# Rebuilt prologue of a two-layer Flamingo kernel: norm statistics on TensorE and ScalarE, another load order, products moved behind the routers, 16-bit tables

## What is computed

```
x = x + tanh(g_xattn[0]) * (_layernorm(x) * rs)     # rs: scan, r = 0.9 r + ctx*ctx along each sequence
x = x + tanh(g_ffn[0])   * _L0_ffn_ref(_layernorm(x), Wg, W_in, W_out)
x = x + tanh(g_xattn[1]) * _L1_xattn_ref(_layernorm(x), ctx, ctx, Wq, bq, Wk, bk, Wv, bv, mask, 1)
x = x + tanh(g_ffn[1])   * _L1_ffn_ref(_layernorm(x), gate_w, w1, w2)

# _L0_ffn_ref: S = 2048 tokens, E = 8 experts, K = 2, capacity C = 640
logits = xf @ Wg;  probs = softmax(logits);  top_vals, top_idx = top_k(probs, K)
loc = place of the token in its expert's list (cumsum of one-hots);  keep = loc < C
buf[e, loc] = token row;  hid = buf @ W_in;  hid = gelu(a) * g;  out_e = hid @ W_out
y = sum over K of out_e[e, loc] * gates
```

## Time and profile before

| | us |
|---|---|
| three runs | 569.64, 570.64, 571.45 |
| median | 570.64 |
| span of the profiled execution | 573.6 |
| TensorE busy in that span | 532.9 (93%) |
| first expert product starts | 76.33 |

### The profile page before, as it was taken

One profiled execution on the slowest core, in us unless ns is written; L12 is line 12 of the kernel. 1 busy time (PEld: TensorE's weight loads), 2 busy tenths in 40 slices (PEclk: granted clock), 3 DMA queues, 4 the chain that ended last, 5 costly groups with the idle time before them and its releaser, 6 DMA issues.

```text
span 573.6 us, 12551 instructions
## 1 busy us (share of the span) xinstructions
PE 532.9 (93%) x4079; PEld 508.9 (89%) x4080; DVE 335.6 (59%) x796; ACT 321.8 (56%) x670; POOL 251.9 (44%) x284
## 2 busy tenths in 40 slices
PE   2899889999999999998996989999999999999993
PEld 1789789999999999986785879999999999999993
DVE  2888845765655675475677865464626463543631
ACT  3573345665656675435577646565646574654742
POOL 2400366664455542314000354556565546654654
PEclk9997699999999999979999899999999999999998
DMA  8944253445245443362033343644454545362333
GB/s 251 382 172 149 74 160 105 152 153 169 91 152 172 119 160 110 119 221 75 0 110 129 77 157 69 191 118 113 113 122 96 143 110 119 48 193 45 42 51 44
DMA packets 52454, 72.76 MB, mean 127 GB/s; under 512 B 7200, under 2 KB 43936, under 8 KB 52416
## 3 DMA queue, kind: packets, MB, share of 16 engines
q1 hardware_dynamic: 40752, 50.34, 26.7%
q0 software_dynamic: 11664, 21.94, 17.2%
HBM read 51.54 MB, written 20.73 MB: 126 GB/s over the span
## 4 chain that ended last, share of the span: by engine, by line
PE 80%; DVE 9%; DMA 4%; ACT 3%; issue 2%; POOL 1%; DVEq 0%; SPq 0%; POOLq 0%; ACTq 0%
PE PA L1684 27%; PE PD L1684 18%; PE PC L1684 17%; PE PB L1515 3%; PE PC L1515 2%; PE PD L1515 2%; PE PB L1696 2%; DMA xg<-xn_rows,row_x 2%; PE PB L1873 2%; DVE stats L990 1%; DMA cx<-ctx 1%; PE PA L1515 1%; PE PA L1549 1%; PE PB L1509 1%; DVE xs L1043 1%
## 5 line engine op out<-in xcount | busy, mean ns | idle before, releaser
L1684 PE MATMUL PA<-xhi,whi 128*128 128x256 f32 (+1 forms) x440 | 128.6, 292 | 4.2 <-issue 2.1
L1684 PE MATMUL PA<-xhi,wlo 128*128 128x256 f32 (+1 forms) x440 | 125.8, 286 | 0.0
L1684 PE MATMUL PA<-xlo,whi 128*128 128x256 f32 (+1 forms) x440 | 125.7, 286 | 0.0
L1250 DVE TENSOR_TENSOR hlo<-cT_all,hhi 128x512 fp32r<-128x512 f32 x78 | 54.2, 694 | 111.8 <-ACT hhi L937 111.7
L935 ACT ACTIVATE cT_all<-PA 128x512 f32<-128x512 f32 x78 | 46.6, 597 | 93.2 <-PE PA L1684 93.1
L609 POOL DMA_INDIRECT out<-ys,row_o x38 | 63.5, 1670 | 75.6 <-DVE ys L1456 41.5
L1684 PEld LDWEIGHTS PA<-xhi,whi 128*128 128x128 f32 x440 | 84.2, 191 | 5.6 <-issue 4.5
L1684 PEld LDWEIGHTS PA<-xlo,whi 128*128 128x128 f32 x440 | 84.2, 191 | 0.0
L1684 PEld LDWEIGHTS PA<-xhi,wlo 128*128 128x128 f32 x440 | 84.1, 191 | 0.0
L1684 PE MATMUL PD<-whi,hhi 128*128 128x256 f32 x284 | 81.1, 285 | 0.4 <-DVE wlo L1202 0.4
L1684 PE MATMUL PD<-whi,hlo 128*128 128x256 f32 x284 | 80.4, 283 | 0.0
(11 more groups left out here) (269 smaller groups left out, 1205.6 us busy)
## 6 DMA issues: line engine op xcount, KB each, us to landing
raw<-w SPq DMA_DIRECT2D x16, 1024.0 KB, 5.7
raw<-L_ffn_W_in SPq DMA_DIRECT2D x8, 1024.0 KB, 5.2
raw<-L_ffn_W_out SPq DMA_DIRECT2D x8, 512.0 KB
y_rows<-ys SPq DMA_DIRECT2D x8, 512.0 KB, 8.0
xn_rows<-xn SPq DMA_DIRECT2D x8, 512.0 KB, 3.5
xs<-x SPq DMA_DIRECT2D x4, 512.0 KB, 6.5
cx<-ctx SPq DMA_DIRECT2D x4, 512.0 KB, 7.0
ys<-y_rows SPq DMA_DIRECT2D x4, 512.0 KB, 4.6
```

The lines of the kernel that those rows point to most:

```text
L1250: return dve.tensor_tensor(dst, src, hi.bitcast(F32), ALU.subtract)
L1684: mm = pe.matmul(dst, a[k], b[k], start=(first and k == 0 and a is lhs_hi and b is rhs_hi), stop=(last and k == n - 1 and a is lhs_lo))
```

## The change

- **Norm statistics of layer 0's second norm.** The router's weights get a ninth column of -1/256, so `rows_router` also gives minus the mean. ACT squares the rows with that mean as bias and sums them (`squares1`), then takes the root (`root1`). `norm_stats(1, q)` on DVE goes.
- **Normalising.** POOL makes the coefficients and normalises quads 0 and 1, DVE quads 2 and 3 (`normalised1`, the first behind `one_hots(0)`, the second behind `pick`); ACT did all four.
- **Squares.** DVE makes the context squares of quad 0, POOL those of 1 to 3.
- **Loads.** The two gate vectors come ahead of the constants; the attention weights come behind all rows and context, the router weights (`wg`, with a semaphore of their own) behind quad 1. `W_in` of expert 0 is loaded ahead of the stores of the normed rows.
- **PE's order.** The routers come first. `weights`, `context(0)`, `value_weights`, `value_gates(0)` and `values(0)` stand around and behind `ranks(0)`, ahead of `invert(0)`; `value_gates(1)` and `values(1)` stand between and behind the transposes of the first gathered tiles. Idle products: 8, 4, 4, 4 and one after each gathered tile, where 4, 5, 11, 6, 9 and five stood. The retention products use two PSUM tiles in turn.
- **Tables.** `maps` compares 16-bit numbers with a 16-bit table in which eight copies of each number lie side by side. So the one-hots lie with the group innermost, and `invert` reads its operands with a step of eight elements (16 bytes). Both layers use it.

```diff
                 if q == 0:
+                    sp.dma_start(gts[:, 0:2], g_xattn.partition_broadcast(P)).then_inc(g_in, 16)
+                    sp.dma_start(gts[:, 2:4], g_ffn.partition_broadcast(P)).then_inc(g_in, 16)
                     sp.dma_start(cf[:, :], cf_d).then_inc(cf_in, 16)
                 sp.dma_start(cx[:, q * QB:(q + 1) * QB, :],
...
+                if q == 1:
+                        sp.dma_start(wg[:, n, :, 0:E], w.rearrange("(c p) e -> p c e", p=P)).then_inc(wg_in, 16)
+            for n, w in enumerate((wq, wk, wvT)):
+                sp.dma_start(wqkv[:, n, :, :], w.rearrange("(c p) d -> p c d", p=P)).then_inc(small_in, 16)
+            for n, b in enumerate((bq, bk, bvc)):
+                sp.dma_start(bqk[:, n, :], b).then_inc(small_in, 16)
+            sp.dma_start(bvb[:, :], bv.partition_broadcast(P)).then_inc(small_in, 16)
...
+            sp.wait_ge(ret_done, NQ)
+            load(0, 0, True)
             for q in range(NQ):
-                if q == NQ - 1:
-                    sp.wait_ge(ret_done, NQ)
-                    load(0, 0, True)
-                sp.wait_ge(xn_ready, XN[1, q])
+                sp.wait_ge(xn1_ready[q], 1)
...
+            pool.wait_ge(cf_in, 16)
+            pool.tensor_copy(number_table[:, :, :], c("iota").unsqueeze(2).broadcast_to([P, P, PART]))
+            pool.tensor_copy(slot16[:, :], c("slot")).then_inc(table_ready, 1)
+            for t in range(1, NQ):
...
+            for q in range(NQ):
+                m = place(1, q)
+                pool.wait_ge(sd_ready, ROOT[1, q])
+                pool.tensor_tensor(nmr[:, m, :], lg[:, q * QB:(q + 1) * QB, E], rstd[:, m, :], ALU.mult)\
+                    .then_inc(coef1_ready, 1)
+                if q < 2:
+                    pool.wait_ge(coef1_ready, q + 1)
+                    for b in range(QB):
+                        ins = pool.tensor_scalar(xn[:, q % 2, b, :], xs[:, q * QB + b, :], rstd[:, m, b:b + 1],
+                                                 nmr[:, m, b:b + 1], ALU.mult, ALU.add)
...
+            def squares1(q):
+
+                act.wait_ge(lg_used, q + 1)
+                for b in range(QB):
+                    ins = act.activation(junk1[:, b, :], xs[:, q * QB + b, :], ACT.Square,
+                                         bias=lg[:, q * QB + b, E:E + 1], accum_out=mv[:, place(1, q), b, 1:2])
+                ins.then_inc(square1_ready, 1)
+
+            def root1(q):
+                act.wait_ge(square1_ready, q + 1)
+                root(1, q, scale=1.0 / D)
...
+            def normalised1(q):
+
+                m = place(1, q)
+                dve.wait_ge(coef1_ready, q + 1)
+                dve.wait_ge(xn_out0[q % 2], 16 * (q // 2))
+                for b in range(QB):
+                    ins = dve.tensor_scalar(xn[:, q % 2, b, :], xs[:, q * QB + b, :], rstd[:, m, b:b + 1],
+                                            nmr[:, m, b:b + 1], ALU.mult, ALU.add)
+                ins.then_inc(xn1_ready[q], 1)
...
+            dve.wait_ge(ctx_in[0], 16)
+            dve.tensor_tensor(cx2[:, 0], cx[:, 0:QB, :], cx[:, 0:QB, :], ALU.mult).then_inc(square0_ready, 1)
...
+                link(dve.scalar_tensor_tensor(low16[:, :], smi[:, 2, :], -float(P), smi[:, 0, :], ALU.mult, ALU.add))
...
+            def maps(layer):
+
+                def over_parts(x):
+                    return x[:, :].rearrange("p (m g) -> p m g", g=PART).unsqueeze(2).broadcast_to([P, MAP_PARTS, NA, PART])
+
+                dve.tensor_tensor(oha, over_parts(high16), number_table[:, 0:NA, :].unsqueeze(1)
+                                  .broadcast_to([P, MAP_PARTS, NA, PART]), ALU.is_equal).then_inc(oha_ready, 1)
                 dve.wait_ge(oha_ready, layer + 1)
-                dve.tensor_tensor(by_slot, oha, slot_wide[:, :, :], ALU.mult)\
-                    .then_inc(slot_ready, 1)
...
-                    dve.tensor_tensor(ohb[:, at, :], smi[:, 1, at].unsqueeze(2).broadcast_to([P, NG // MAP_PARTS, P]),
-                                      c("iota").unsqueeze(1).broadcast_to([P, NG // MAP_PARTS, P]), ALU.is_equal)\
+                    dve.tensor_tensor(ohb[:, n, :, :], low16[:, n * PART:(n + 1) * PART].unsqueeze(1)
+                                      .broadcast_to([P, P, PART]), number_table[:, :, :], ALU.is_equal)\
...
             one_hots(0)
+            normalised1(2)
             dve.wait_ge(rank_done, 1)
             pick()
             link(dve.tensor_scalar(sm[:, 1, :], smi[:, 0, :], float(CAP), float(64), ALU.is_ge, ALU.mult))
             link(dve.scalar_tensor_tensor(sm[:, 2, :], eidx[:, :], float(CT), smi[:, 2, :], ALU.mult, ALU.add))
-            link(dve.tensor_tensor(sm[:, 3, :], sm[:, 1, :], sm[:, 2, :], ALU.add))
+            link(dve.tensor_tensor(high16[:, :], sm[:, 1, :], sm[:, 2, :], ALU.add))
+            normalised1(3)
             dve.wait_ge(zero_out, 16 * K * NQ)
-            maps(0, sm[:, 3, :])
-            link(dve.tensor_tensor(lg[:, :, :], lg[:, :, :], top[:, :, 0:1].broadcast_to([P, NB, E]), ALU.subtract))
+            dve.wait_ge(table_ready, 1)
+            maps(0)
+            link(dve.tensor_tensor(lg[:, :, 0:E], lg[:, :, 0:E], top[:, :, 0:1].broadcast_to([P, NB, E]), ALU.subtract))
...
             for k in range(DC):
                 win0(0, k)
+            value_gates(0)
             value_gates(1)
...
+            def busy(count, at=PC[:, 0, 0:P]):
...
+            busy(8, early_fill)
             retention(0)
-            context(0)
-            busy(4)
-            values(0)
+            router_sums()
             retention(1)
             rows(0)
-            router_sums()
-            weights(0)
             retention(2)
-            weights(1)
+            rows_router(0)
+            retention(3)
             rows(1)
-            retention(3)
-            rows_router(0)
-            busy(5, PA)
+            pe.wait_ge(ret_used, 3)
+            busy(4, early_fill)
+            rows_router(1)
             rows(2)
-            rows_router(1)
-            busy(11, PA)
+            busy(4, early_fill)
+            rows_router(2)
             rows(3)
-            rows_router(2)
+            busy(4, early_fill)
             rows_router(3)
-            value_weights()
-            busy(6, PB)
 
             def ranks(layer):
 
@@ -1659,22 +1689,24 @@
 
                 pe.wait_ge(slot_ready, layer + 1)
                 for g in range(NG):
-                    if g % (NG // MAP_PARTS) == 0:
-                        pe.wait_ge(map_ready, layer * MAP_PARTS + g // (NG // MAP_PARTS) + 1)
-                    mm = pe.matmul(PD[:, 0, 128:128 + MAP_BLOCKS * NA], ohb[:, g, :], rhs_a[:, g, :], start=(g == 0),
...
+                    if g % PART == 0:
+                        pe.wait_ge(map_ready, layer * MAP_PARTS + g // PART + 1)
+                    mm = pe.matmul(PD[:, 0, 128:128 + MAP_BLOCKS * NA],
+                                   ohb[:, g // PART, :, g % PART], rhs_a[:, g // PART, :, g % PART],
+                                   start=(g == 0), stop=(g == NG - 1))
...
+            weights(0)
             pe.wait_ge(cb_ready, 1)
             ranks(0)
+            weights(1)
+            context(0)
+            value_weights()
             value_gates(0)
+            values(0)
+            invert(0)
             context(1)
-            busy(9)
-            invert(0)
-            value_gates(1)
-            values(1)
-            pe.wait_ge(evac_done, EV1["v", 1])
 
             def exact(dst, lhs_hi, lhs_lo, rhs_hi, rhs_lo, first=True, last=True):
 
@@ -1696,7 +1728,7 @@
...
-            xt0(0, 0, 0, 0, filler=2)
+            pe.wait_ge(evac_done, EV1["cT", 1])
+            xt0(0, 0, 0, 0, filler=1)
+            value_gates(1)
             xt0(0, 0, 0, 1, filler=1)
+            values(1)
+            pe.wait_ge(evac_done, EV1["v", 1])
             pe.wait_ge(target0_ready, 1)
             with pe.Fori(0, E // 2) as i:
```

239 lines of the change are left out of this document (108 added, 131 removed).

## The result

The changed kernel takes 590.96 us (median of four runs, 586.58 to 595.71), the kernel before 570.14 beside it: a ratio of 1.0329, 95% interval 1.0281 to 1.0377. A run more than 1.5% above the fastest of its kernel, like the one at 595.71 here, 588.77 in e2 and single ones at 598 to 1405 in e5, e14 and e17, counts in the median but not in the ratio. The forecast was 567.5. The profiled execution (589.59 us, span 587.8) has its first expert product at 88.30, where 73.2 was forecast and 76.33 stood before.

What follows compares the result with a forecast made beforehand. The prologue was taken as bound by latency, a chain of waits to the first expert product. Ranks at 41.7, first gather at 54.9 plus 18.3 gave 73.2 against 76.33; 570.64 - 3.1 = 567.5 us, range 563.5 to 574.0.

Steps and rivals of the forecast that it cites:

- Part one, ranks at 41.7: From the start to the rank products' end: VectorE's shortened list ends them at 41.7 us, 11.1 earlier.
- 1.6 where a GpSimd square holds up a DVE operation: Ahead of the ranks: 1.6 us of waiting added to VectorE's list for GpSimd squares.
- a rival for the routers: Clock falls already between the routers: start +6.3 us, 3.2 slower than before, 573.8; chance 0.20.
- Part two, "all at full clock": From ranks to inversion: TensorE's products sum to 10.1 us at full clock, so the inversion starts at 51.8.
- one for the values only (+2.2): Clock falls during quad 0's value products: they take 5.6 us, not 3.7; +2.2, 569.7; chance 0.20.
- Strided reads: Inversion's 16-byte-step operand reads: forecast no cost; rival of half pace, +2.5 us in sum, 570.0, chance 0.10.
- twice the time as the other end: Upper bound for the inversion's strided reads: its products take twice as long, +1.7 us in layer 0.
- In layer 1 I allowed 0.8: Under the strided-read rival, layer 1's inversion delays things by 0.8 us, as the list had 0.3 to spare.
- Part three, R + 18.3: From the first gather, R, to the first expert product: 18.3 us, where it was 11.9.
- I counted 6.4 us for it: Behind the first gather: lost cover for quad 1's products gives back 6.4 of the 9.6 us won there.
- 3.0 above: The profiled execution of the kernel before was taken as 3.0 us above its runs' median when setting the forecast.

Runs made afterwards that it cites:

- e2: Changed kernel with its 16-bit tables laid out with two groups side by side instead of eight: 584.84 us, ratio 1.013.
- e5: Kernel before with only 16-bit tables in pairs (two groups side by side) added: 572.96 us, ratio 0.9949.
- e14: e12 with ScalarE doing the first expert's weight conversions, exponentials and table load while waiting for quad 0's value products: 566.73 us, ratio 0.9946.
- e17: e14 with e8's order behind the inversion on TensorE and ScalarE: 572.27 us, ratio 1.0049.
- e9: e8 with late-needed products reordered behind the inversion, ScalarE's list to match, and a few idle products fewer: 572.78 us, ratio 1.0024.
- e12: e9 with each of GpSimd's three squares split in four: 569.70 us, ratio 1.0002.
- e15: Changed kernel with only GpSimd's squares split in four: 585.28 us, ratio 1.0244.
- e4: Changed kernel with idle products in TensorE's gaps and the first half of the weight products moved behind the ranks: 590.31 us, ratio 1.0277.
- e1: Changed kernel with the tables slot by slot again, so the inversion reads contiguous operands: 582.69 us, ratio 1.015.
- e13: Changed kernel in its own order behind the ranks, with tables in pairs, squares split in four and idle products: 574.80 us, ratio 1.0088.
- e18: The kernel of e14 run again, beside e17 on one chip: 566.85 us, ratio 0.9933.
- e3: Kernel before with only the change's 16-bit tables, eight groups side by side: ratio 1.013.
- e6: Changed kernel with the inversion again ahead of quad 0's value gates and products: 589.09 us, ratio 1.0227.
- e7: e6 with the tables in pairs: 581.96 us, ratio 1.0112.
- e10: e9 without the added idle products and with half of the weight products ahead of the ranks: 576.66 us, ratio 1.011.
- e16: Kernel before with tables in pairs, ten more idle products and squares split in four: 572.33 us, ratio 1.0029.
- e8: e7 with more idle products than e4 and half of the weight products behind the ranks: 576.76 us, ratio 1.0020.

## Why the prediction was wrong

**Part one, ranks at 41.7: off by 4.0.** The list of VectorE was right. The failed term is "1.6 where a GpSimd square holds up a DVE operation": 3.9 us in the changed kernel, since each of the three squares caught an operation. That is 2.3 too little. The split alone brought the ranks forward by 2.33 on e9's kernel (e12) and by 3.2 on the changed one (e15), so its price depends on what stands beside it. The rest, some 1.7, is the clock on the way to the ranks, which I had as a rival for the routers: transposes took 1.97 and 1.95 for 1.04 to 1.07 at 18.73 and 32.52, `weights(0)` 2.05 for 1.11 ahead of the ranks. e9, with idle products and `weights(0)` behind the ranks, has them 1.9 sooner (43.80 for 45.71); the two are not separated. With both mended the ranks end at 41.47.

**Part two, "all at full clock": off by 7.8.** This is the main failed step: the sum of 10.1 between ranks and inversion took 17.9, at a granted clock of 0.50. I had two rivals on the clock, one for the values only (+2.2), one for the routers (+6.3), both too small: neither took in weight products, transposes, value weights and gates behind the ranks, all of which ran at 0.50. (VectorE's list there has a slip of 0.1, 42.8 for 42.9, which changes nothing: its maps were not waited for.) The rows before had shown it, 0.62 at 46 to 48 behind narrow products, but there only part of it lay on the path, and I priced it for quad 0's values alone. The change put all those products on the path, and the same clock then cost 7.8. e4 shows 10.4 at a mostly held clock.

**Strided reads: off by 3.8 in layer 0 and 1.7 in layer 1.** I took nothing, with twice the time as the other end; it is 3.6 times (5.5 for 1.5) at full clock. The Trainium skill's rule (SBUF — State Buffer, "Door 1: The DMA port swizzle"), 16-byte lines and a penalty for each access that crosses to a new one, agrees with e1 and e2: one element of a line read is slow, four of eight are not. I had it in hand and gave it 0.10. In layer 1 I allowed 0.8; from the first map to the gather 11.0 us pass for 9.3 before (8.6 in e1), and the list, not the store, comes last; 1.2 of that is hidden, as the maps begin so much sooner behind the experts.

**Part three, R + 18.3: right.** It was R + 18.40 in the changed kernel (first gather at 69.90) and R + 18.1 in e13, and by the way that was forecast: gates 3.42, values 5.40, both at half clock. That cover is lost by this order was right too: I counted 6.4 us for it, and e17 against e18 gives 5.4, early conversions included.

**The base.** The forecast subtracted from the median what the profiled execution, "3.0 above", showed. I compared its span with the median of times. In all runs here 1.8 us lie between a run's span and its time, so it was some 4.8 above. The traces differ by 14.2 in span, the medians by 20.8.

**Where the 23.5 us between forecast and result lie:** ranks 4.0, clock behind them 7.8, inversion 3.8, less 0.5 at the gathers; 0.5 more to the first gather of layer 1 and 1.7 behind it, which I did not follow up; together 17.3 by the traces. The other 6 are the profiled execution of the kernel before, slower than its median by 4.8, and that of the changed kernel, faster than its own by 1.4.

## What to carry over

Work that runs in the shade of another engine may run at half clock unseen; before moving it onto the path, price it at the clock that its own rows show, with all narrow products around it. A layout that speeds the writer must be priced at the reader too: here two groups side by side gave VectorE its full gain and TensorE its full pace. And late-needed work belongs behind the issue of the gathers, not behind the first landing: that order, with ScalarE's list drawn up to match, was worth 1%.

## What the runs showed of the hardware that I had not expected

- 16-bit operands of 128x128 weights and 128x92 at a step of 16 bytes: 0.17 us a product, 5.6 us for 32 at either clock (e3, e6). At a step of 4 bytes 32 took 1.52 at full clock (e2) and 2.61 at half (e7); without a step 1.50 at full clock (e1).
- A GpSimd instruction of 1.89 stretches a four-element VectorE one from 0.15 to 1.14; in pieces of a quarter, to 0.43. The four pieces took 2.32 in all, 0.43 more than the whole.
- Behind three to four us without a product, the first expert's products ran for a while at 0.47 for 0.31 in e9, e10, e12 and e17, and so they did behind 2.6 in e14. But they did so in e16 too, behind 0.88, and did not behind 3.02 in the changed kernel, e7 and e8. So the gap alone does not decide it, and what does is open.
- Idle products did not hold the clock surely. e12 and e13 have the same lists up to the ranks. e12 shows 1.00 in every window up to 56, e13 0.77 at 28 to 32 and 0.81 at 32 to 36, and the same transposes took 1.07 in the one and 1.70 in the other:

```profile
29.87 1.07 PE L1547 MATMUL PB<-cf,xs 128*128 128x128 f32 x8
```

```profile
29.87 1.70 PE L1546 MATMUL PB<-cf,xs 128*128 128x128 f32 x8
```

- e14 and e18 are one kernel: at 44 to 48 the one shows 1.00 and the other 0.65, and their first expert products come at 70.99 and 72.66. So profiled runs of one kernel differ by several us in the start, and a mechanism is better read from the durations than from the end time of one trace.
